# Routing by expert choice: a threshold search on two engines instead of one

## The chip, the cores and the metric

The kernel runs on one core of a Trainium2 chip. Its engines are TensorE (PE in the profile: matmuls, with PEld for weight loads), VectorE (DVE), ScalarE (ACT), GpSimd (POOL) and SyncE (SP, which issues DMAs). They run their own instruction streams and meet at semaphores. The metric is the device time of one execution in microseconds, the median of some runs.

## The reference

The program is one transformer layer on 4096 tokens of 256 features: linear attention with random features, a feed-forward block, and a mixture of 8 experts. The part that matters here is how the experts choose their tokens. `x` has 8 x 512 tokens:

```
scores = softmax(xf @ gate_w.T, axis=-1)        # 4096 tokens x 8 experts
vals, idx = top_k(scores.T, k)                  # k = 4096 / 8 = 512 tokens for each expert
y = xf[idx]                                     # gathered rows, normalised
h = gelu(y @ fc1[e].T + b1[e]);  out = (h @ fc2[e].T + b2[e]) * vals
xf = xf.at[idx].add(out)                        # scattered back
x = x + layernorm(xf)
```

So for each expert the 512 largest of 4096 scores are wanted, exactly, and ties at the threshold go to the first tokens.

## The kernel before, in words

Everything is one launch, written by hand with one instruction stream for each engine and named semaphores between them. First come eight batches of 512 tokens through attention, feed-forward and gate, as a software pipeline of three stages; `batches` writes batches 0 to 2 and the tail as straight-line code and the middle ones as a hardware loop. Then comes the selection, then `experts`: expert 0, a loop over the middle ones, and the last two. At the end the sum is normalised and written.

The selection works like this. The gate's scores lie in `sc`; TensorE turns them (L1353) into PSUM tile `pA[0]`, so that each of the 128 partitions holds 256 scores: 16 partitions for each of the 8 experts. VectorE copies them to `S` (L1098), which lies in the free buffer `kp`, and makes a bfloat16 copy of their upper halves, `S_hi` (L1101). A score is positive, so its f32 bits as an integer are in the same order as the score. The search settles three bits of the threshold in each of ten rounds. In a round

- VectorE counts, for each of 7 candidates, how many scores of the partition are at least the candidate (L1108, a compare with an accumulator, so each is followed by a read of the accumulator); the first four rounds use `S_hi`, the other six `S`;
- TensorE sums the counts over the 16 partitions of an expert with the 0/1 matrix `blockones` (L1627) into `pA[1]`;
- VectorE compares the sums with 512 (L1115), scales the number of candidates that passed by the step (L1117), and makes the next 7 candidates (L1118), the threshold so far (L1119) and the next step (L1120). `Steps.link` puts a wait behind an instruction, so the next one starts only when it is done; `Steps.put` doesn't.

On VectorE the rounds are two hardware loops with two rounds in a body, on TensorE one loop. Behind the search VectorE counts once more, above the cut and equal to it (L1131, L1132), and turns the counts into places, one-hot matrices and at last row numbers `idx` (to L1176). GpSimd then gathers the rows of expert 0 (L799), and only then can expert 0 start: TensorE turns the rows (L1353), ScalarE applies the layer norm's scale and shift (L616, Identity), and the first hidden products follow (L1382), with Gelu on ScalarE (L630).

What sets the order of the work around the search: SyncE issues the weights of expert 0 (`kp<-fc1T`, `w<-fc2T`, 1 MB each) as soon as the last batch's buffers are free, and the following experts' weights behind `idx_ready`. GpSimd wrote the selection's constants once, in front of the batches (`selection_constants`, from L673). ScalarE has nothing to do between the last batch and L616.

Of the kernel before, what the change touches and what calls it, by code (L numbers as in the profile page):

```python
# [6 lines left out]
ALU = mybir.AluOpType  # L7
# [10 lines left out]
P = 128  # L18
# [11 lines left out]
EPS_K = 1e-4  # L30
N_CONST = 14
N_WFF = 13
N_SEL = 13
LN_EPS = 1e-5
LNS = 5
NORM = DH ** -0.25
# [5 lines left out]
ROW = D + E  # L42
GT = KEEP // P

ROUNDS, CANDS = 10, 7
HI_ROUNDS = 4
SA, SB = 32, 16
SR = P // SA
LQ = 4
# [48 lines left out]
def build(nc, video, WqT, bq, WkT, bk, WvT, bv, WoT, bo, projT, W1T, b1, W2T, b2, g2, be2, g3, be3,  # L98
          gateT, ln_w, ln_b, fc1T, b1s, fc2T, b2s, out, stop=None):
    with ExitStack() as ctx:  # L100
# [10 lines left out]
        def features_of(t):  # L111
# [83 lines left out]

        kp_f, qe_f, qp_f = (a[:].rearrange("p a b -> p (a b)") for a in (kp, qe, qp))
        S, gt, eq, gin, ein, place = (kp_f[:, k * SEGW:(k + 1) * SEGW] for k in range(6))
        flags = qe_f[:, 8 * SEGW:(8 + CANDS) * SEGW].rearrange("p (k j) -> p k j", k=CANDS)

        flags_hi, S_hi = (qe_f[:, k * SEGW:(k + w) * SEGW].bitcast(BF16) for k, w in ((8, CANDS // 2 + 1), (15, 1)))  # L200
        flags_hi, S_hi = flags_hi[:, 0:CANDS * SEGW].rearrange("p (k j) -> p k j", k=CANDS), S_hi[:, 0:SEGW]
        dig_a, dig_b = (kp_f[:, 7 * SEGW:8 * SEGW].bitcast(F16)[:, k * SEGW:(k + 1) * SEGW].rearrange("p (e c s) -> p e c s", c=C, e=E)
                        for k in range(2))
        placei, digi_a, digi_b = (qe_f[:, k * SEGW:(k + 1) * SEGW].bitcast(I32).rearrange("p (c e s) -> p c e s", c=C, e=E)
                                  for k in (8, 9, 10))
        thr = sb("thr", [P, 1], U32)
        step = sb("step", [P, CANDS], U32)
        nstep = sb("nstep", [P, CANDS], U32)
        base = sb("base", [P, CANDS], U32)
        cand = sb("cand", [P, CANDS], U32)  # L210
        cnt = sb("cnt", [P, CANDS])
        passed = sb("passed", [P, CANDS])
        npass = sb("npass", [P, 1])
        up = sb("up", [P, 1], U32)
        ones_row = sb("ones_row", [P, SEGW])
        blockones = sb("blockones", [P, P])
        blockbelow = sb("blockbelow", [P, P])
# [94 lines left out]
        x1_out, xf_out, y_out, sc_out = sem("x1_out"), sem("xf_out"), sem("y_out"), sem("sc_out")  # L312
        dve_n, dve_a, dve_f, dve_u = sem("dve_n"), sem("dve_a"), sem("dve_f"), sem("dve_u")
        sel_const, sel_step, s_turned, s_ready = sem("sel_const"), sem("sel_step"), sem("s_turned"), sem("s_ready")
        cnt_ready, tot_ready, dve_s, dve_r = sem("cnt_ready"), sem("tot_ready"), sem("dve_s"), sem("dve_r")
        pair_ready, off_ready, place_ready, place_turned = sem("pair_ready"), sem("off_ready"), sem("place_ready"), sem("place_turned")
        oneb_ready, onea_ready, onehot_ready, ids_ready, rbd_ready, spread_ready, idx_ready = (
            sem("oneb_ready"), sem("onea_ready"), sem("onehot_ready"), sem("ids_ready"), sem("rbd_ready"), sem("spread_ready"), sem("idx_ready"))
# [10 lines left out]
            sem("olv_ready"), sem("olp_ready"))  # L329

        STEPS_N, STEPS_A, STEPS_F, STEPS_U = 1, 7, 1, 7
        SEL_STEPS = 7

        vid_d = video.rearrange("(b t p) d -> b p t d", t=TT, p=P)
        x1_t = x1_d.rearrange("(b t p) d -> b p t d", t=TT, p=P)
# [125 lines left out]
        def _(act):  # L461
# [188 lines left out]
        def _(pool):  # L650
# [21 lines left out]
            def selection_constants():  # L672
                nc.gpsimd.memset(ones_row[:], 1.0).then_inc(sel_const, 1)  # L673
                nc.gpsimd.memset(zero4[:], 0.0).then_inc(sel_const, 1)

                for k in range(CANDS):
                    nc.gpsimd.memset(step[:, k:k + 1], (k + 1) << 27).then_inc(sel_const, 1)
                nc.gpsimd.memset(thr[:], 0).then_inc(sel_const, 1)

                for m in (blockones, blockbelow, spread, rmask):  # L680
                    nc.gpsimd.memset(m[:], 1.0).then_inc(sel_step, 1)
                nc.gpsimd.iota(iota_row[:], [[1, SA]], base=0, channel_multiplier=0).then_inc(sel_step, 1)
                pool.wait_ge(sel_step, 5)
# [165 lines left out]
        def _(dve):  # L849
# [244 lines left out]
            done.link(nc.vector.tensor_scalar(pmod[:], pint[:], SR - 1, None, ALU.bitwise_and))  # L1094
            done.link(nc.vector.tensor_copy(pmodf[:], pmod[:]))
            done.link(nc.vector.tensor_scalar(rmask[:], iotaf[:, 0:SR], pmodf[:, 0:1], None, ALU.is_equal))
            dve.wait_ge(s_turned, 1)
            nc.vector.tensor_copy(S, pA[0][:, 0:SEGW]).then_inc(s_ready, 1)  # L1098
            dve.wait_ge(s_ready, 1)

            done.link(nc.vector.tensor_copy(S_hi, S.bitcast(BF16).rearrange("p (j h) -> p j h", h=2)[:, :, 1]))  # L1101

            def search(rd, s, fl):


                ss = Steps(dve, dve_r, SEL_STEPS, rd)
                for k in range(CANDS):
                    nc.vector.tensor_scalar(fl[:, k], s, cand[:, k:k + 1].bitcast(F32), None, ALU.is_ge, ALU.add,  # L1108
                                            accum_out=cnt[:, k:k + 1]).then_inc(cnt_ready, 1)

                ss.link(nc.vector.tensor_scalar(nstep[:], step[:], 3, None, ALU.logical_shift_right))
                ss.put(nc.vector.tensor_tensor(base[:], nstep[:], thr[:].to_broadcast([P, CANDS]), ALU.bitwise_or))
                dve.wait_ge(tot_ready, rd + 1)

                ss.link(nc.vector.tensor_scalar(passed[:], pA[1][:, 0:CANDS], KEEP - 0.5, None, ALU.is_ge, ALU.add,  # L1115
                                                accum_out=npass[:]))
                ss.link(nc.vector.tensor_scalar(up[:], step[:, 0:1], npass[:, 0:1], None, ALU.mult))  # L1117
                ss.put(nc.vector.tensor_tensor(cand[:], base[:], up[:].to_broadcast([P, CANDS]), ALU.bitwise_or))  # L1118
                ss.put(nc.vector.tensor_tensor(thr[:], thr[:], up[:], ALU.bitwise_or))  # L1119
                ss.link(nc.vector.tensor_copy(step[:], nstep[:]))  # L1120
                ss.end()

            done.link(nc.vector.tensor_copy(cand[:], step[:]))
            with dve.Fori(0, HI_ROUNDS // 2) as r2:
                search(r2 * 2, S_hi, flags_hi)
                search(r2 * 2 + 1, S_hi, flags_hi)
            with dve.Fori(HI_ROUNDS // 2, ROUNDS // 2) as r2:
                search(r2 * 2, S, flags)
                search(r2 * 2 + 1, S, flags)
            cut = thr[:, 0:1].bitcast(F32)  # L1130
            nc.vector.tensor_scalar(gt, S, cut, None, ALU.is_gt, ALU.add, accum_out=pair_cnt[:, 0:1])  # L1131
            nc.vector.tensor_scalar(eq, S, cut, None, ALU.is_equal, ALU.add, accum_out=pair_cnt[:, 1:2]).then_inc(pair_ready, 1)  # L1132
            dve.wait_ge(pair_ready, 1)
            nc.vector.tensor_tensor_scan(gin, ones_row[:], gt, 0.0, ALU.mult, ALU.add)
            nc.vector.tensor_tensor_scan(ein, ones_row[:], eq, 0.0, ALU.mult, ALU.add)
# [157 lines left out]
        def _(pe):  # L1293
# [436 lines left out]
```

## Time and profile before

| | us |
|---|---|
| median of 3 runs | 970.05 (969.35 to 970.36) |
| the profiled execution, its own time | 970.41 |
| its span, first to last instruction | 968.6 |
| busy: PE 762.2, DVE 595.6, ACT 410.6, POOL 352.9 | |
| mean granted TensorE clock | 0.900 of full speed |

The stages follow each other: batches to about 630, the search to 677, placing to 698, gather and the turning of the first rows to 715, experts to about 929, the last normalisation to the end. The page cuts the span into 40 slices of 24.2 us; a digit is the busy share of an engine in a slice, in tenths. The busy share of an engine over the whole span says little about a single stage; the rows below are read by stage.

### The profile page before, as it was taken

How to read it: one execution, taken by the hardware profiler on the slowest of the kernel's cores; microseconds unless marked ns; L12 is line 12 of the kernel's file. 1: busy time of each engine (PE TensorE's matmuls, PEld its weight loads, DVE VectorE, ACT ScalarE, POOL GpSimd, SP SyncE). 2: the span in 40 equal slices, each digit the busy share in tenths (PEclk: the TensorE clock that was granted, in tenths of full speed). 3: DMA queues.
4: the chain of work that ended last, by engine and by line, in shares of the span. 5: the costliest groups of instructions: out<-in, count | busy, mean ns of one | idle time of the engine just before them, and what ended most of it. 6: DMA issues, size and time to landing. Idle time of an engine off the chain costs nothing.

```text
span 968.6 us, 15201 instructions
## 1 busy us (share of the span) xinstructions
PE 762.2 (79%) x5561; PEld 581.5 (60%) x5561; DVE 595.6 (61%) x1426; ACT 410.6 (42%) x594; POOL 352.9 (36%) x299
## 2 busy tenths in 40 slices
PE   5578999999999999999999967211459989999900
PEld 2345856767767758668577656211348888888800
DVE  2722735857857957848758562588836656666445
ACT  2632634735636536637447321100045434455324
POOL 3136333514416405425335151100134444544346
PEclk9798999999999999999999979555569999999955
DMA  7000010011011020110100102220053555555274
GB/s 208 1 23 1 1 45 1 2 66 46 23 44 44 22 84 3 48 61 0 65 23 1 66 23 83 71 94 0 7 169 92 153 132 170 138 132 135 31 213 150
DMA packets 61530, 64.63 MB, mean 67 GB/s; under 512 B 9264, under 2 KB 58160, under 8 KB 61488
## 3 DMA queue, kind: packets, MB, share of 16 engines
q1 hardware_dynamic: 54384, 55.37, 17.4%
q0 software_dynamic: 6144, 8.52, 5.0%
q8 instruction: 27, 0.44, 0.2%
q10 hardware_dynamic: 960, 0.17, 0.1%
q14 instruction: 15, 0.12, 0.0%
HBM read 42.95 MB, written 21.10 MB: 66 GB/s over the span
## 4 chain that ended last, share of the span: by engine, by line
PE 62%; DVE 13%; DMA 6%; ACT 6%; POOL 6%; issue 5%; POOLq 0%; DVEq 0%; SPq 0%; ACTq 0%
PE pF L1382 10%; PE pX L1660 10%; PE pF L1424 9%; PE pA L1368 6%; PE pA L1375 5%; PE pX L1464 5%; DMA xg<-row_scratch,idx_g 4%; PE pX L1393 4%; PE pA L1353 3%; DVE qe L1108 3%; PE pX L1382 3%; POOL xg L799 2%; PE pA L1434 2%; PE pF L1477 2%; PE pF L1353 2%
## 5 line engine op out<-in xcount | busy, mean ns | idle before, releaser
L1424 PE MATMUL pF<-w,h 128*128 128x256 f32 x512 | 116.0, 380 | 0.0
L1424 PEld LDWEIGHTS pF<-w,h 128*128 128x128 f32 x512 | 95.6, 190 | 13.8 <-issue 1.4
L719 POOL TENSOR_SCALAR ve<-mv 128x4 f32<-128x4 f32 x40 | 9.1, 228 | 247.0 <-DVE mv L861 246.4
L807 POOL DMA_INDIRECT acc_scratch<-at,idx_s x32 | 51.6, 1613 | 107.3 <-DVE at L1216 100.6
L799 POOL DMA_INDIRECT xg<-row_scratch,idx_g x32 | 47.3, 1478 | 99.0 <-issue 86.0
L630 ACT ACTIVATE h<-pX,b1cur 128x512 f32<-128x512 f32 x64 | 44.1, 690 | 88.9 <-DVE b1cur L1227 75.4
L1660 PE MATMUL pX<-w_lo,h_hi 128*128 128x256 f32 x256 | 73.7, 288 | 0.8 <-issue 0.8
L1660 PE MATMUL pX<-w_hi,h_lo 128*128 128x256 f32 x256 | 73.0, 285 | 0.0
L1660 PE MATMUL pX<-w_hi,h_hi 128*128 128x256 f32 x256 | 72.9, 285 | 0.0
L867 DVE TENSOR_SCALAR z<-z,mv,rstd 128x256 f32<-128x256 f32 x64 | 62.3, 1034 | 7.0 <-POOL rstd L721 7.0
L479 ACT ACTIVATE h<-pF,b1c 128x512 f32<-128x512 f32 x64 | 44.2, 691 | 48.4 <-PE pF L1382 48.4
L1199 DVE TENSOR_TENSOR h_lo<-h,h_hi 128x512 fp32r<-128x512 f32 x64 | 42.9, 690 | 30.5 <-ACT h_hi L622 30.5
L1382 PE MATMUL pF<-x2T_hi,w_lo 128*128 128x512 f32 x128 | 55.1, 430 | 1.4 <-DVE x2T_lo L957 1.4
L1382 PE MATMUL pX<-x2T_hi,w_lo 128*128 128x512 f32 x128 | 51.8, 405 | 2.8 <-DVE x2T_lo L1248 2.8
L1382 PE MATMUL pX<-x2T_lo,w_hi 128*128 128x512 f32 x128 | 51.6, 403 | 0.0
L1382 PE MATMUL pF<-x2T_hi,w_hi 128*128 128x512 f32 x128 | 51.5, 403 | 0.0
L1382 PE MATMUL pX<-x2T_hi,w_hi 128*128 128x512 f32 x128 | 51.4, 401 | 0.0
L1382 PE MATMUL pF<-x2T_lo,w_hi 128*128 128x512 f32 x128 | 51.2, 400 | 0.0
L1660 PEld LDWEIGHTS pX<-w_lo,h_hi 128*128 128x128 f32 x256 | 49.7, 194 | 1.4 <-issue 1.4
L888 DVE TENSOR_REDUCE mxk<-kp 128x16 f32<-128x1024 f32 x32 | 37.3, 1209 | 21.4 <-ACT kp L489 21.4
L1660 PEld LDWEIGHTS pX<-w_hi,h_lo 128*128 128x128 f32 x256 | 49.7, 194 | 0.0
L1660 PEld LDWEIGHTS pX<-w_hi,h_hi 128*128 128x128 f32 x256 | 49.6, 194 | 0.0
(260 smaller groups left out, 1860.0 us busy)
## 6 DMA issues: line engine op xcount, KB each, us to landing
kp<-fc1T SPq DMA_DIRECT2D x8, 1024.0 KB, 7.9
w<-fc2T SPq DMA_DIRECT2D x8, 1024.0 KB, 8.0
xin<-video SPq DMA_DIRECT2D x8, 512.0 KB, 3.9
x<-video SPq DMA_DIRECT2D x8, 512.0 KB, 4.5
x_scratch<-x SPq DMA_DIRECT2D x8, 512.0 KB, 2.9
acc_scratch<-xf SPq DMA_DIRECT2D x8, 512.0 KB, 3.0
row_scratch<-y SPq DMA_DIRECT2D x8, 512.0 KB, 3.0
qp<-x_scratch SPq DMA_DIRECT2D x2, 1024.0 KB, 10.5
```

The source lines that it names most:

```text
L479: nc.scalar.activation(dst, pF[n % 2][:], func, **kw).then_inc(done, 1)
L630: nc.scalar.activation(h[:, n, :], pM[n % M_SLOTS], ACT.Gelu_apprx_tanh, bias=b1cur[:, n:n + 1]).then_inc(he_ready, 1)
L799: pool.indirect_dma_start(xg[:, g, :], None, row_d, bass.IndirectOffsetOnAxis(ap=idx_g[:, g:g + 1], axis=0)).then_inc(gathered, 16)
L807: pool.indirect_dma_start(acc_d, bass.IndirectOffsetOnAxis(ap=idx_s[:, g:g + 1], axis=0), og[:, g, :], None, compute_op=ALU.add).then_inc( ...
L867: ins = nc.vector.tensor_scalar(dst[:, t, :], src[:, t, :], mv[k][:, t, 0:1], rstd[k][:, t:t + 1], ALU.subtract, ALU.mult)
L1353: return nc.tensor.transpose(dst, src, ident[:])
L1368: ins = nc.tensor.matmul(dst[:, t2 * D:(t2 + 1) * D], xt[:, k, tok(2 * m + t2)], w[:, k, :], start=(k == 0), stop=(k == ks - 1))
L1375: ins = nc.tensor.matmul(dst[:], w[:, k, tok(n)], xt[:, k, :], start=(k == 0), stop=(k == ks - 1))
L1382: ins = nc.tensor.matmul(dst[:], w_[:, k, tok(n)], x_[:, k, :], start=(m == 0), stop=(m == len(parts) - 1))
L1424: ins = nc.tensor.matmul(slots[m][:, half * D:(half + 1) * D], h[:, k, tok(2 * m + half)], w2[:, k, :], start=(k == 0), stop=(k == FC - 1))
L1464: ins = nc.tensor.matmul(pXall[:, a, :], w_[rows], x_[rows], start=(n == 0), stop=(n == 2), tile_position=(32 * a, 0))
L1660: ins = nc.tensor.matmul(pM[2 + m][:, t2 * D:(t2 + 1) * D], h_[:, k, tok(2 * m + t2)], w_[:, k, :], start=(k == 0 and j == 0), stop=(k == ...
```

## The change

The search still settles three bits in each of ten rounds, with 7 candidates. What differs:

- The scores become numbers. The upper bits of the score (shifted right by 15) are cast to f32 as `S_top` and searched in rounds 0 to 4; then the low 15 bits, scaled by 2^-15, are joined to what is left of `S_top` above the threshold found, and this `S` is searched in rounds 5 to 9. Candidates lie half a step between the values, so none is ever equal to a score.
- VectorE counts 4 candidates (scores below the candidate), ScalarE 3, as the sum of Sign(candidate - score) over the row, with an accumulator. For a sum of signs the limit differs; the limits stand in `limit`.
- The decision is a compare with `limit`, a reduce, one instruction for the next candidates (which ScalarE awaits, `cand_ready`), and one for the threshold `below`. The first candidates of each half are made before the search.
- TensorE waits for both engines' counts (`cnt_ready`, `sgn_ready`).
- The rounds are straight-line code on VectorE, ScalarE and TensorE.
- ScalarE runs one small Sign before the search and one small Gelu behind it, into `spare`.
- GpSimd sets four small constants where it set eight.

```diff
-ROUNDS, CANDS = 10, 7
-HI_ROUNDS = 4
+ROUNDS, CANDS, CANDS_V = 10, 7, 4
+HI_ROUNDS = ROUNDS // 2
+LOW_BITS = 15
+STEP = [float(1 << 3 * (HI_ROUNDS - 1 - r)) for r in range(HI_ROUNDS)] + [2.0 ** (-3 * (r + 1)) for r in range(HI_ROUNDS)]
+BELOW = (-0.5, -0.5 * STEP[ROUNDS - 1])
...
+            act.wait_ge(sel_const, N_SEL)
+            nc.scalar.activation(spare[:], zero4[:, 0:1], ACT.Sign)
+            for rd in range(ROUNDS):
+                act.wait_ge(s_ready, 1 if rd < HI_ROUNDS else 3)
+                act.wait_ge(cand_ready, rd + 1 if rd < HI_ROUNDS else rd)
+                now = cand_low if rd == HI_ROUNDS else cand
+                for j in range(CANDS - CANDS_V):
+                    k = CANDS_V + j
+                    nc.scalar.activation(signs[:, j], S_top if rd < HI_ROUNDS else S, ACT.Sign, bias=now[:, k:k + 1], scale=-1.0,
+                                         accum_out=cnt[:, k:k + 1]).then_inc(sgn_ready, 1)
+            nc.scalar.activation(spare[:], zero4[:, 0:1], ACT.Gelu_apprx_tanh)
...
-                for k in range(CANDS):
-                    nc.gpsimd.memset(step[:, k:k + 1], (k + 1) << 27).then_inc(sel_const, 1)
-                nc.gpsimd.memset(thr[:], 0).then_inc(sel_const, 1)
+                for k in range(2):
+                    nc.gpsimd.memset(thr[:, k:k + 1], BELOW[k]).then_inc(sel_const, 1)
+
+                nc.gpsimd.memset(limit[:, 0:CANDS_V], SEG * SEGW - KEEP + 0.5).then_inc(sel_const, 1)
+                nc.gpsimd.memset(limit[:, CANDS_V:CANDS], SEG * SEGW - 2 * KEEP + 0.5).then_inc(sel_const, 1)
...
+            nc.vector.tensor_scalar(cand[:], iotaf[:, 1:CANDS + 1], STEP[0], BELOW[0], ALU.mult, ALU.add).then_inc(cand_ready, 1)
+            done.link(nc.vector.tensor_scalar(cand_low[:], iotaf[:, 1:CANDS + 1], STEP[HI_ROUNDS], BELOW[1], ALU.mult, ALU.add))
             dve.wait_ge(s_turned, 1)
-            nc.vector.tensor_copy(S, pA[0][:, 0:SEGW]).then_inc(s_ready, 1)
+            done.link(nc.vector.tensor_scalar(bits_top, pA[0][:, 0:SEGW].bitcast(I32), LOW_BITS, None, ALU.arith_shift_right))
+            nc.vector.tensor_copy(S_top, bits_top).then_inc(s_ready, 1)
             dve.wait_ge(s_ready, 1)
...
+            ss = Steps(dve, dve_r, 0, 0)
+            for rd in range(ROUNDS):
+                half = rd // HI_ROUNDS
+                last_of_half = rd % HI_ROUNDS == HI_ROUNDS - 1
+                scores, now = S if half else S_top, cand_low if rd == HI_ROUNDS else cand
+                below = thr[:, half:half + 1]
+                for k in range(CANDS_V):
+                    nc.vector.tensor_scalar(flags[:, k], scores, now[:, k:k + 1], None, ALU.is_lt, ALU.add,
+                                            accum_out=cnt[:, k:k + 1]).then_inc(cnt_ready, 1)
+                if rd == 0:
+                    done.link(nc.vector.tensor_scalar(bits_low, pA[0][:, 0:SEGW].bitcast(I32), (1 << LOW_BITS) - 1, None, ALU.bitwise_and))
+                    nc.vector.tensor_scalar(S_low, bits_low, 2.0 ** -LOW_BITS, BELOW[0], ALU.mult, ALU.add).then_inc(s_ready, 1)
+                if not last_of_half:
+                    ss.link(nc.vector.tensor_scalar(kstep[:], iotaf[:, 1:CANDS + 1], STEP[rd + 1], below, ALU.mult, ALU.add))
                 dve.wait_ge(tot_ready, rd + 1)
+                ss.link(nc.vector.tensor_tensor(passed[:], pA[1][:, 0:CANDS], limit[:], ALU.is_le))
+                ss.link(nc.vector.tensor_reduce(npass[:], passed[:], AX_X, ALU.add))
+                if not last_of_half:
+                    nc.vector.scalar_tensor_tensor(out=cand[:], in0=npass[:].to_broadcast([P, CANDS]), scalar=STEP[rd], in1=kstep[:],
+                                                   op0=ALU.mult, op1=ALU.add).then_inc(cand_ready, 1)
+                ss.link(nc.vector.tensor_scalar(below, npass[:], STEP[rd], below, ALU.mult, ALU.add))
+                if rd == HI_ROUNDS - 1:
+                    dve.wait_ge(s_ready, 2)
+                    nc.vector.scalar_tensor_tensor(out=S, in0=S_top, scalar=below, in1=S_low, op0=ALU.subtract, op1=ALU.add).then_inc(s_ready, 1)
+                    dve.wait_ge(s_ready, 3)
+                elif not last_of_half:
+                    dve.wait_ge(cand_ready, rd + 2 if rd < HI_ROUNDS else rd + 1)
+            done.link(nc.vector.tensor_scalar(cut[:], thr[:, 1:2], BELOW[1], None, ALU.subtract))
...
-            with pe.Fori(0, ROUNDS) as rd:
-                pe.wait_ge(cnt_ready, (rd + 1) * CANDS)
+            for rd in range(ROUNDS):
+                pe.wait_ge(cnt_ready, (rd + 1) * CANDS_V)
+                pe.wait_ge(sgn_ready, (rd + 1) * (CANDS - CANDS_V))
                 nc.tensor.matmul(pA[1][:, 0:CANDS], blockones[:], cnt[:], start=True, stop=True).then_inc(tot_ready, 1)
```

## Rows read from the trace of the kernel before

**Rows 1.** The page, the span in 40 slices of 24.2 us.
```profile
DVE  2722735857857957848758562588836656666445
ACT  2632634735636536637447321100045434455324
PEclk9798999999999999999999979555569999999955
```

**Rows 2.** Busy us (instructions): PE, PEld, DVE, ACT, POOL; then clock, DMA share, GB/s.
```profile
631.00:677.00 46.00, 5.95 (x20) 5.01 (x20) 38.51 (x221) 0.00 (x0) 0.00 (x0) 0.50 0.14 49
```

**Rows 3.** Timeline of VectorE in rounds 5 to 7: start, duration, line; and the search's end.
```profile
649.95 0.48 DVE L1108 TENSOR_SCALAR_CACHE_REDUCE qe<-kp,cand 128x256 f32<-128x256 f32 x1 [0.38 <-DVE step L1120]
650.35 0.08 DVE L1108 DVE_READ_ACCUMULATOR qe<-kp,cand 128x1 f32 x1
...
652.75 0.09 DVE L1108 DVE_READ_ACCUMULATOR qe<-kp,cand 128x1 f32 x1
...
653.52 0.17 DVE L1115 TENSOR_SCALAR_CACHE_REDUCE passed<-pA 128x7 f32<-128x7 f32 x1 [0.40 <-PE pA L1627]
...
653.73 0.22 DVE L1117 TENSOR_SCALAR up<-step,npass 128x1 uint32<-128x1 uint32 x1
653.98 0.17 DVE L1118 TENSOR_TENSOR cand<-base,up 128x7 uint32<-128x7 uint32 x1
654.06 0.15 DVE L1119 TENSOR_TENSOR thr<-thr,up 128x1 uint32<-128x1 uint32 x1
...
654.33 0.48 DVE L1108 TENSOR_SCALAR_CACHE_REDUCE qe<-kp,cand 128x256 f32<-128x256 f32 x1
...
659.12 0.48 DVE L1108 TENSOR_SCALAR_CACHE_REDUCE qe<-kp,cand 128x256 f32<-128x256 f32 x1 [0.44 <-DVE step L1120]
...
677.23 0.48 DVE L1131 TENSOR_SCALAR_CACHE_REDUCE kp<-kp,thr 128x256 f32<-128x256 f32 x1 [0.23 <-DVE step L1120]
```

**Rows 4.** Timeline of VectorE at the start of the search.
```profile
630.14 0.42 DVE L1098 COPY kp<-pA 128x256 f32<-128x256 f32 x1
630.60 0.29 DVE L1101 COPY qe<-kp 128x256 bf16<-128x256 bf16 x1
...
631.35 0.48 DVE L1108 TENSOR_SCALAR_CACHE_REDUCE qe<-qe,cand 128x256 bf16<-128x256 bf16 x1 [0.25 <-DVE cand L1123]
```

**Rows 5.** VectorE's groups by form: count, busy us, mean ns of one, idle before.
```profile
L1117 DVE TENSOR_SCALAR up<-step,npass 128x1 uint32<-128x1 uint32 x10 | 2.1, 215 | 0.4
...
L1144 DVE SCALAR_TENSOR_TENSOR kp<-kp,offs 128x256 f32<-128x256 f32 x1 | 0.5, 485 | 0.0
...
L1043 DVE TENSOR_REDUCE lmx<-lg 128x4 f32<-128x32 f32 x2 | 0.4, 186 | 0.1
```

**Rows 6.** ScalarE's groups by form over the span, same columns.
```profile
L538 ACT ACTIVATE y<-x,ny,ry 128x256 f32<-128x256 f32 x32 | 16.6, 588 | 61.3 <-DVE ny L1003 55.8 <-issue 5.5
...
L474 ACT ACTIVATE kT<-pA,bqk 128x512 f32<-128x512 f32 x16 | 11.0, 687 | 52.0 <-PE pA L1375 52.0
...
L474 ACT ACTIVATE v<-pA 128x512 f32<-128x512 f32 x16 | 9.6, 597 | 17.3 <-PE pA L1368 17.3
...
L603 ACT ACTIVATE lg<-lg 128x32 f32<-128x32 f32 x8 | 1.8, 231 | 7.3 <-DVE lg L1044 7.3
```

**Rows 7.** Timeline of ScalarE behind the search.
```profile
711.71 0.78 ACT L616 ACTIVATE aT<-pX,lnb_c,lnw_c 128x512 f32<-128x512 f32 x1 [83.02 <-PE pX L1353]
...
718.33 1.28 ACT L630 ACT_TABLE_LOAD   x1 [3.85 <-PE pX L1382]
719.63 0.69 ACT L630 ACTIVATE h<-pX,b1cur 128x512 f32<-128x512 f32 x1
```

**Rows 8.** DMAs from 625 to 700: issues, KB each, us to landing.
```profile
w<-fc2T SPq DMA_DIRECT2D x1, 1024.0 KB, 7.9
```

**Rows 9.** The chain of waits from 610 to 740: start, duration.
```profile
715.35 13.61 PE pX L1382 x48
```

**Rows 10.** Who waited for whom: us in total, times, the longest.
```profile
DVE st L857 <- issue: 0.9, 3, 0.3
```

More of the change, by code:

```diff
@@ L32 @@
 N_WFF = 13
-N_SEL = 13
+N_SEL = 9
 LN_EPS = 1e-5
@@ L197, in build @@
         S, gt, eq, gin, ein, place = (kp_f[:, k * SEGW:(k + 1) * SEGW] for k in range(6))
-        flags = qe_f[:, 8 * SEGW:(8 + CANDS) * SEGW].rearrange("p (k j) -> p k j", k=CANDS)
-        flags_hi, S_hi = (qe_f[:, k * SEGW:(k + w) * SEGW].bitcast(BF16) for k, w in ((8, CANDS // 2 + 1), (15, 1)))
-        flags_hi, S_hi = flags_hi[:, 0:CANDS * SEGW].rearrange("p (k j) -> p k j", k=CANDS), S_hi[:, 0:SEGW]
+        S_top, S_low = (kp_f[:, k * SEGW:(k + 1) * SEGW] for k in (6, 4))
+        flags = qe_f[:, 8 * SEGW:(8 + CANDS_V) * SEGW].rearrange("p (k j) -> p k j", k=CANDS_V)
+        signs = qe_f[:, (8 + CANDS_V) * SEGW:15 * SEGW].rearrange("p (k j) -> p k j", k=CANDS - CANDS_V)
+        bits_top, bits_low = (kp_f[:, k * SEGW:(k + 1) * SEGW].bitcast(I32) for k in (1, 2))
         dig_a, dig_b = (kp_f[:, 7 * SEGW:8 * SEGW].bitcast(F16)[:, k * SEGW:(k + 1) * SEGW].rearrange("p (e c s) -> p e c s", c=C, e=E)
@@ L205, in build @@
                                   for k in (8, 9, 10))
[L206 to L210, printed above, removed]
+        thr = sb("thr", [P, 2])
+        kstep = sb("kstep", [P, CANDS])
+        cand = sb("cand", [P, CANDS])
+        cand_low = sb("cand_low", [P, CANDS])
+        limit = sb("limit", [P, CANDS])
+        cut = sb("cut", [P, 1])
+        spare = sb("spare", [P, 1])
         cnt = sb("cnt", [P, CANDS])
@@ L213, in build @@
         npass = sb("npass", [P, 1])
-        up = sb("up", [P, 1], U32)
         ones_row = sb("ones_row", [P, SEGW])
@@ L314, in build @@
         sel_const, sel_step, s_turned, s_ready = sem("sel_const"), sem("sel_step"), sem("s_turned"), sem("s_ready")
-        cnt_ready, tot_ready, dve_s, dve_r = sem("cnt_ready"), sem("tot_ready"), sem("dve_s"), sem("dve_r")
+        cnt_ready, sgn_ready, tot_ready, dve_s, dve_r, cand_ready = (
+            sem("cnt_ready"), sem("sgn_ready"), sem("tot_ready"), sem("dve_s"), sem("dve_r"), sem("cand_ready"))
         pair_ready, off_ready, place_ready, place_turned = sem("pair_ready"), sem("off_ready"), sem("place_ready"), sem("place_turned")
@@ L331, in build @@
         STEPS_N, STEPS_A, STEPS_F, STEPS_U = 1, 7, 1, 7
-        SEL_STEPS = 7
         vid_d = video.rearrange("(b t p) d -> b p t d", t=TT, p=P)
@@ L1099, in _ @@
+            nc.vector.tensor_copy(S_top, bits_top).then_inc(s_ready, 1)
             dve.wait_ge(s_ready, 1)
[L1101 to L1108, printed above, removed]
-                                            accum_out=cnt[:, k:k + 1]).then_inc(cnt_ready, 1)
-                ss.link(nc.vector.tensor_scalar(nstep[:], step[:], 3, None, ALU.logical_shift_right))
-                ss.put(nc.vector.tensor_tensor(base[:], nstep[:], thr[:].to_broadcast([P, CANDS]), ALU.bitwise_or))
-                dve.wait_ge(tot_ready, rd + 1)
[L1115 to L1131, printed above, removed]
@@ L1132, in _ @@
-            nc.vector.tensor_scalar(eq, S, cut, None, ALU.is_equal, ALU.add, accum_out=pair_cnt[:, 1:2]).then_inc(pair_ready, 1)
+            ss = Steps(dve, dve_r, 0, 0)
[6 more added lines that the diff above has]
+                    nc.vector.tensor_scalar(flags[:, k], scores, now[:, k:k + 1], None, ALU.is_lt, ALU.add,
+                                            accum_out=cnt[:, k:k + 1]).then_inc(cnt_ready, 1)
+                if rd == 0:
[3 more added lines that the diff above has]
+                    ss.link(nc.vector.tensor_scalar(kstep[:], iotaf[:, 1:CANDS + 1], STEP[rd + 1], below, ALU.mult, ALU.add))
+                dve.wait_ge(tot_ready, rd + 1)
+                ss.link(nc.vector.tensor_tensor(passed[:], pA[1][:, 0:CANDS], limit[:], ALU.is_le))
[10 more added lines that the diff above has]
+                    dve.wait_ge(cand_ready, rd + 2 if rd < HI_ROUNDS else rd + 1)
@@ L1133, in _ @@
+            done.link(nc.vector.tensor_scalar(cut[:], thr[:, 1:2], BELOW[1], None, ALU.subtract))
+            nc.vector.tensor_scalar(gt, S, cut[:, 0:1], None, ALU.is_gt, ALU.add, accum_out=pair_cnt[:, 0:1])
+            nc.vector.tensor_scalar(eq, S, cut[:, 0:1], None, ALU.is_equal, ALU.add, accum_out=pair_cnt[:, 1:2]).then_inc(pair_ready, 1)
             dve.wait_ge(pair_ready, 1)
@@ L1622, in _ @@
             ins.then_inc(s_turned, 1)
-            with pe.Fori(0, ROUNDS) as rd:
-                pe.wait_ge(cnt_ready, (rd + 1) * CANDS)
+            for rd in range(ROUNDS):
+                pe.wait_ge(cnt_ready, (rd + 1) * CANDS_V)
+                pe.wait_ge(sgn_ready, (rd + 1) * (CANDS - CANDS_V))
                 nc.tensor.matmul(pA[1][:, 0:CANDS], blockones[:], cnt[:], start=True, stop=True).then_inc(tot_ready, 1)
             pe.wait_ge(pair_ready, 1)
-            pe.wait_ge(s_ready, 1)
+            pe.wait_ge(s_ready, 2)
             nc.tensor.matmul(pA[0][:, 0:2], blockbelow[:], pair_cnt[:], start=True, stop=True)
```

## The prediction

> **What bounds the kernel now.** I read the page's slices first, then the busy times by stage, then the timeline of the search, then the rows of the engine that is to take work over. The slices show, near two thirds of the span, VectorE at 8 and ScalarE at 0 with TensorE's granted clock at 5 [rows 1]. The stage gives its size [rows 2]: in the 46 us from 631 to 677 VectorE is busy 38.5 us, TensorE 6, ScalarE and GpSimd nothing. That is the threshold search: one dependent chain through VectorE and TensorE, so every microsecond of it is a microsecond of the span, and all later work (placing, gather, experts) starts from its result.
>
> One round [rows 3]: the first count starts at 649.95; the reads of the first and the seventh accumulator stand at 650.35 and 652.75, six spacings, so counts follow each other by 0.40, and the last is read at 652.84: 2.89 = 6 x 0.40 + 0.49. TensorE's block sum and its way back take 0.68, to L1115 at 653.52. The decision (L1115, L1117 to L1120) takes 0.81, to the next count at 654.33: 4.38 us in all. Every second round also turns the loop: 659.12 lies 4.79 behind 654.33, with 0.44 idle in front of it. Ten rounds go from 631.35 [rows 4] to the count for the cut at 677.23 [rows 3].
>
> **The change, part by part.** All of it is counted on this chain.
>
> (a) Three of seven counts leave VectorE. Four take 3 x 0.40 + 0.49 = 1.69, 1.20 less per round. The bfloat16 copy of the scores goes too; it bought nothing: a count of it lasts 0.48 [rows 4], one of f32 0.48 [rows 3].
>
> (b) The decision. L1115's replacement is a compare of 7 columns without an accumulator, as short as L1118 (0.17 [rows 3]), and then a reduce; the nearest reduce is 186 ns for 32 columns [rows 5]. A dependent instruction starts some 0.04 behind its predecessor (L1118 behind L1117 [rows 3]), so each takes 0.21. The next candidates are one instruction, 0.17. Behind them the new base, one column with a pointer scalar like L1117 (215 ns [rows 5]), may start 0.08 after the candidates, as L1119 does behind L1118 [rows 3], and is awaited. So the counts start 0.42 + 0.08 + 0.22 + 0.04 = 0.76 behind the compare, where it is 0.81 now. kstep stands before the wait for TensorE and fits beside its 0.68.
>
> (c) No loop turn: the pause of about 0.4 in every second round goes.
>
> A round of VectorE is then 0.76 + 1.69 + 0.68 = 3.13 us.
>
> (d) ScalarE's three signs. It has candidates 0.42 + 0.17 + 0.03 = 0.62 behind the compare. No row has a Sign with an accumulator. The nearest is the 128x256 activation with two pointer operands: 588 ns, 16.6 us for 32 busy, so 0.52 each where they overlap [rows 6]. One pointer less saves 687 - 597 = 90 ns [rows 6]. So a Sign lasts 0.50 and follows by 0.43 at most, and I take 0.42. Lower bound of the three: 2 x 0.42 + 0.50 = 1.34, the accumulator free. Upper bound: each also pays a separate read as dear as the shortest activation, 231 ns [rows 6], and nothing overlaps: 3 x (0.50 + 0.23) = 2.19. The nearest row in kind is VectorE's read of an accumulator, 0.08 [rows 3]; it gives 1.34 + 3 x 0.08 = 1.58, and that I take. ScalarE is then ready 0.62 + 1.58 = 2.20 behind the compare and VectorE 0.76 + 1.69 = 2.45: ScalarE is hidden by 0.25. It comes last only if the three take more than 1.83.
>
> (e) Start. Two tables of candidates stand in front of the wait for the turned scores: up to 0.08 + 0.17 + 0.04 = 0.29, and I hide nothing of it. The shift starts at 630.43 instead of 630.14 [rows 4]; from PSUM it costs L1098's 0.42 + 0.04, the cast L1101's 0.29 + 0.05. First count: 631.23, against 631.35 now.
>
> (f) First round: between counts and decision stand the low 15 bits (0.46, from PSUM), their scaling (0.27) and kstep (0.27): 1.00 where 0.68 would do, so +0.32. Middle: behind the fifth decision the scores are put together once, with a pointer scalar (485 ns at L1144 [rows 5]): 0.21 + 0.21 + 0.26 + 0.53 = 1.21 instead of 0.76, so +0.45. End: 0.21 + 0.21 + 0.26 + 0.19 = 0.87 to the count for the cut.
>
> Sum: first compare at 631.23 + 1.69 + 0.68 + 0.32 = 633.92; nine rounds more, 9 x 3.13 + 0.45 = 28.62, to 662.54; + 0.87 gives 663.41. Now it is 677.23, so 13.8 us go.
>
> (g) Side work at nothing. TensorE runs the same ten sums, with a second wait in front of each; what is queued behind each is only the next sum. GpSimd sets constants once, ahead of the batches, four small ones fewer; its next work there waits for other engines, so I take 0. ScalarE was idle for 83.02 us before its first instruction behind the search, at 711.71 [rows 7]; 30 signs and two small activations in about 34 us fit there, and only that instruction is queued behind them. Expert 0's weights (1 MB in 7.9 us [rows 8]) are issued at the start of the search and needed behind it: some 20 us of cover stay even if they wait for each other.
>
> (h) The Gelu table. Now its load of 1.28 us stands before the first hidden activation, at 718.33 [rows 7]; the spare Gelu moves it behind the search. I count no gain: TensorE's 48 matmuls of that stretch stand in the chain of waits as one piece of 13.61 us from 715.35 on, without a wait for ScalarE [rows 9]. Between -1.3 and 0, I take 0. Whether Sign is in the table now loaded (it serves Copy, Relu, Square and Exp) no row shows; if not, the spare Sign costs from 0 to 1.3 once, less what lies between ScalarE's last exponential and the first candidate; I take 0.
> The Trainium skill, "ScalarE: Activation LUTs", section "What ACT_TABLE_LOAD costs", puts a drain of some 1.38 us on top of the 1.28. Here the next activation starts at 719.63, 0.02 behind the load [rows 7]: measurement and page differ. By the page each warm-up would end 1.4 later; the Gelu's would still lie inside the idle 83 us and the sum would stay, while a Sign in a table of its own would cost up to 2.7 once.
>
> The profiled execution took 970.41 (span 968.6), the median run 970.05. From the profiled one the sum is 956.6, from the median 956.2. Every term is at its row's shortest spacing, so I predict 956.6.
>
> **Rivals.**
> 1. ScalarE comes last. For it: the accumulator's price is unseen, and the margin is 0.25 in 3.1. Against: only a read dearer than about 0.16 decides it. At the upper bound a round is 0.62 + 2.19 + 0.68 = 3.49, so 8 x 0.36 + 0.5 in the middle + 0.2 in the first = 3.6 us of the gain go: 960.2.
> 2. An exposed instruction fetch. The search was a loop on VectorE and TensorE and becomes straight-line code on three engines, while 2 MB of weights are in flight. For it: a transfer among those weights takes 7.9 us to land [rows 8]. Against: the longest idle time of VectorE put down to issue is 0.3 us in the whole span [rows 10], though four of eight batches run as straight-line code. One exposed fetch costs up to 7.9: up to 964.5.
> 3. Slower than before: two such fetches, both within the transfer of the weights and both on the chain, on engines that wait for each other. The price is 2 x 7.9 = 15.8 against 13.8 gained: 972.4. It decides from 6.9 us per fetch; nothing in the trace comes near it.
> 4. The search shortens, but the gain is given back by what follows: the gather, or TensorE's clock. Against: the gather needs only rows that were written before the search, and the granted clock is 5 from the search through the gather either way [rows 1]. The time would be 970.
>
> **How the numbers follow.** Forecast 0.58; rival 1 in some measure 0.28; rival 2 0.09; rival 3 0.03; rival 4 0.02. The range is 955.0 to 961.5: below, the load of 1.3 counted as no gain, and 0.3 for the start; above, ScalarE's upper bound and a small stall. A measurement tells 0.2% (1.9 us) from no change; forecast and rivals 1 and 2 are faster, and of rival 2 a hundredth is worse: 0.94; no change 0.02; slower 0.04.
>
> **What would show it.** In the changed profile: first counts of two rounds 3.13 apart (3.5 by rival 1); TensorE's idle time before the sums put down to VectorE's count, not to ScalarE's sign; Sign rows near 0.50, the last one ended before VectorE's fourth count; the count for the cut 13.8 earlier; no row of the experts changed; the table load near 663. I am wrong if TensorE waits for ScalarE, if the rounds have idle time put down to issue, or if a load appears between signs.

## The result, and the profile after

The changed kernel takes 956.77 us (median of 4 runs, 953.76 to 959.91); the kernel before took 970.2 beside it (4 runs). The ratio is 0.9862, 95% interval 0.9829 to 0.9895. Predicted were 956.6 and a range of 955.0 to 961.5. The profiled execution took 959.91, its span is 957.8.

The same slices as in [rows 1], now 23.9 us each. ScalarE has two 4s where it had 0s behind the batches, and the row of TensorE's clock has one 5 fewer there:

```profile
DVE  2631634875866857857957754657636656566445
ACT  1542553744745635635546513044045434455424
PEclk9789899999999999999999989655569999999955
```

The stage of the search, with the columns of [rows 2]. It is 33 us long where it was 46; TensorE has the same 20 passes in it, ScalarE 62 instructions where it had none:

```profile
633.00:666.00 33.00, 5.95 (x20) 5.01 (x20) 26.04 (x133) 17.32 (x62) 0.00 (x0) 0.52 0.21 70
```

One round, as [rows 3] showed one: start and duration, all engines, from one compare to the next. VectorE and ScalarE read the same scores at the same time, and neither is slower for it: a count lasts 0.48 as in [rows 3], and a Sign lasts 0.49, as the fourth Sign of split_3_4 does with no count beside it:

```profile
639.55 0.17 DVE L1141 TENSOR_TENSOR passed<-pA,limit 128x7 f32<-128x7 f32 x1 [0.62 <-PE pA L1651]
639.75 0.16 DVE L1142 TENSOR_REDUCE npass<-passed 128x1 f32<-128x7 f32 x1
639.94 0.17 DVE L1144 SCALAR_TENSOR_TENSOR cand<-npass,kstep 128x7 f32<-128x7 f32 x1
640.03 0.21 DVE L1146 TENSOR_SCALAR thr<-npass,thr 128x1 f32<-128x1 f32 x1
640.20 0.51 ACT L625 ACTIVATE qe<-kp,cand 128x256 f32<-128x256 f32 x1 [1.58 <-DVE cand L1144]
640.27 0.48 DVE L1132 TENSOR_SCALAR_CACHE_REDUCE qe<-kp,cand 128x256 f32<-128x256 f32 x1
640.62 0.19 ACT L625 ACTIVATION_READ_ACCUMULATOR qe<-kp,cand 128x1 f32 x1
...
640.71 0.49 ACT L625 ACTIVATE qe<-kp,cand 128x256 f32<-128x256 f32 x1
...
641.20 0.49 ACT L625 ACTIVATE qe<-kp,cand 128x256 f32<-128x256 f32 x1
...
641.60 0.19 ACT L625 ACTIVATION_READ_ACCUMULATOR qe<-kp,cand 128x1 f32 x1
641.87 0.08 DVE L1132 DVE_READ_ACCUMULATOR qe<-kp,cand 128x1 f32 x1
641.87 0.23 DVE L1139 TENSOR_SCALAR kstep<-iotaf,thr 128x7 f32<-128x7 f32 x1
642.01 0.59 PE L1651 MATMUL pA<-cnt,blockones 128*128 128x7 f32 x2 [2.57 <-DVE qe L1132]
642.71 0.17 DVE L1141 TENSOR_TENSOR passed<-pA,limit 128x7 f32<-128x7 f32 x1 [0.61 <-PE pA L1651]
```

ScalarE's last read ends at 641.79, VectorE's at 641.95, and TensorE starts at 642.01. The waits say the same: before all ten sums TensorE waited for VectorE, never for ScalarE (us in total, times, the longest).

```profile
PE pA L1651 <- DVE qe L1132: 26.4, 10, 2.9
```

The start of the selection, the start of the search and its end, which answer to [rows 4] and the last row of [rows 3], and the table load behind it:

```profile
632.15 0.15 DVE L1113 TENSOR_SCALAR pmod<-pint 128x1 int32<-128x1 int32 x1
...
633.07 0.42 DVE L1120 TENSOR_SCALAR kp<-pA 128x256 int32<-128x256 int32 x1
633.53 0.29 DVE L1121 CAST kp<-kp 128x256 f32<-128x256 int32 x1
633.86 0.48 DVE L1132 TENSOR_SCALAR_CACHE_REDUCE qe<-kp,cand 128x256 f32<-128x256 f32 x1
...
664.35 1.28 ACT L627 ACT_TABLE_LOAD   x1
665.64 0.20 ACT L627 ACTIVATE spare<-zero 128x1 f32<-128x1 f32 x1
666.02 0.48 DVE L1155 TENSOR_SCALAR_CACHE_REDUCE kp<-kp,cut 128x256 f32<-128x256 f32 x1
```

For all kernels I take the search as the time from the first instruction of the selection (pmod, a fixed point in every version) to the count for the cut. Here it is 666.02 - 632.15 = 33.87 us. In the kernel before the same instruction stood at 629.44:

```profile
629.44 0.15 DVE L1094 TENSOR_SCALAR pmod<-pint 128x1 int32<-128x1 int32 x1
```

so the search took 677.23 - 629.44 = 47.79, and 13.92 us of it are gone. But this execution reached the selection 2.71 us later than that one, 0.4 us are lost behind the search, and 0.3 lie outside the span. So only 10.5 us lie between the two profiled executions; between the medians it is 13.4. The experiments show what those 2.71 us are.

### The profile page after: what moved, and what is told of

Its sections match the earlier page's. It is cut to its first block, busy times and chain, and to the rows that moved or that the text cites. A ratio compares the mean times of both kernels' runs of the same rounds, so it can differ in the third digit from the quotient of the medians.

```text
span 957.8 us, 15109 instructions
## 1 busy us (share of the span) xinstructions
PE 766.5 (80%) x5561; PEld 584.4 (61%) x5561; DVE 582.5 (61%) x1337; ACT 426.5 (45%) x656; POOL 353.2 (37%) x295
## 4 chain that ended last, share of the span: by engine, by line
PE 64%; DVE 13%; ACT 6%; POOL 6%; DMA 5%; issue 4%; POOLq 0%; DVEq 0%; ACTq 0%; SPq 0%
PE pF L1406 10%; PE pX L1684 10%; PE pF L1448 9%; PE pA L1392 6%; PE pA L1399 5%; PE pX L1488 5%; DMA xg<-row_scratch,idx_g 4%; PE pX L1406 4%; PE pX L1417 4%; PE pA L1377 3%; POOL xg L818 2%; PE pA L1458 2%; ACT qp L534 2%; DVE qe L1132 2%; PE pF L1501 2%
## 5 line engine op out<-in xcount | busy, mean ns | idle before, releaser
L1448 PEld LDWEIGHTS pF<-w,h 128*128 128x128 f32 x512 | 95.6, 190 | 13.8 <-issue 1.4
## 6 DMA issues: line engine op xcount, KB each, us to landing
qp<-x_scratch SPq DMA_DIRECT2D x2, 1024.0 KB, 10.5
```

The costliest lines, as they stand in the source:

```text
L1448: ins = nc.tensor.matmul(slots[m][:, half * D:(half + 1) * D], h[:, k, tok(2 * m + half)], w2[:, k, :], start=(k == 0), stop=(k == FC - 1))
```

## The experiments

Each ratio is against the kernel before, timed beside the run: its median was 970.2 for the changed kernel, 970.15 for the runs from changed_again to unroll_only, 970.97 for those from no_gelu_preload to f16_and_base and 969.61 for the last two. "Search" is the stretch just defined; "selection starts" is its first instruction in the profiled execution.

| kernel | median us | ratio, 95% interval | search | selection starts |
|---|---|---|---|---|
| before | 970.15 | | 47.79 | 629.44 |
| changed | 956.77 | 0.9862 (0.9829 to 0.9895) | 33.87 | 632.15 |
| changed_again | 956.69 | 0.9855 (0.9838 to 0.9873) | 33.80 | 631.86 |
| split_7_0 | 968.19 | 0.9981 (0.9967 to 0.9994) | 45.86 | 629.26 |
| split_3_4 | 960.45 | 0.9891 (0.9873 to 0.9908) | 37.91 | 632.34 |
| unroll_only | 967.03 | 0.9974 (0.9955 to 0.9992) | 45.53 | 633.52 |
| no_gelu_preload | 955.76 | 0.9853 (0.9831 to 0.9876) | 33.84 | 631.13 |
| base_not_awaited | 955.88 | 0.9847 (0.9830 to 0.9863) | 32.95 | 630.90 |
| sum_in_f16 | 952.45 | 0.9820 (0.9798 to 0.9842) | 30.21 | 628.63 |
| f16_and_base | 952.43 | 0.9813 (0.9799 to 0.9826) | 29.38 | 631.01 |
| kstep_not_awaited | 957.57 | 0.9870 (0.9850 to 0.9891) | 33.21 | 631.72 |
| all_three | 951.58 | 0.9819 (0.9806 to 0.9833) | 28.77 | 630.77 |

The searches lie 19 us apart. The median less the search is 921.5 to 924.4 in all twelve rows, and 921.5 to 923.1 without kstep_not_awaited: the search accounts for the differences of the medians to that measure.

**changed_again** has no edit.

> The changed kernel once more, for its own spread and for a second trace. Theory A (the whole change of time is the search; the two profiled executions differ by 2.7 us before it because TensorE's clock rose later in the first batch, by chance): the stretch from the shift of the scores to the count for the cut is again 32.95 us, while the time of single executions scatters over some us; median near 956.3. Rival (the change itself delays the batches): the batches end near 631 again and not near 628.5 as in the kernel before.

The search is 33.80, and the median agrees with the first measurement. The selection starts at 631.86, which by itself would speak for the rival; unroll_only decides that below.

**split_7_0**: all seven counts on VectorE. ScalarE's Signs, their limit and TensorE's wait for them are taken out too.

```diff
-ROUNDS, CANDS, CANDS_V = 10, 7, 4
+ROUNDS, CANDS, CANDS_V = 10, 7, 7
...
```

> The changed kernel with all seven counts on VectorE and no Sign on ScalarE. Theory A (what the engines share is what pays): three counts more per round, 3 x 0.40 = 1.20, so 12.0 us more, near 968.5, a round of 4.37. Rival (the shorter decision and the missing loop turns pay, the sharing little): under 962.

```profile
629.26 0.15 DVE L1101 TENSOR_SCALAR pmod<-pint 128x1 int32<-128x1 int32 x1
...
675.12 0.48 DVE L1143 TENSOR_SCALAR_CACHE_REDUCE kp<-kp,cut 128x256 f32<-128x256 f32 x1
```

The search is 45.86, so 11.99 us longer than 33.87, and the time is 968.19. The sharing is worth 12.0 us, as three counts of 0.40 in ten rounds are; the rival falls.

**split_3_4**: three counts on VectorE, four Signs on ScalarE.

```diff
-ROUNDS, CANDS, CANDS_V = 10, 7, 4
+ROUNDS, CANDS, CANDS_V = 10, 7, 3
```

> The changed kernel with three counts on VectorE and four signs on ScalarE. Theory A (ScalarE sits just below the point where it decides): four signs end 0.65 + 3 x 0.495 + 0.39 + 0.19 = 2.72 behind the compare, so TensorE waits for ScalarE and a round is 2.72 + 0.69 = 3.41 instead of 3.17: some 2.4 us slower than the changed kernel, near 959. Rival (ScalarE has room, VectorE decides): 0.40 less per round, some 4 us faster, near 952.5.

The sign of the expectation was right and its size too small: 3.8 us slower than the changed kernel, not 2.4; a round is 3.55, not 3.41. The timeline of a round, from its reduce on:

```profile
640.88 0.16 DVE L1142 TENSOR_REDUCE npass<-passed 128x1 f32<-128x7 f32 x1 [0.23 <-DVE passed L1141]
...
642.60 0.09 DVE L1132 DVE_READ_ACCUMULATOR qe<-kp,cand 128x1 f32 x1
...
643.22 0.19 ACT L625 ACTIVATION_READ_ACCUMULATOR qe<-kp,cand 128x1 f32 x1
643.52 0.50 PEld L1651 LDWEIGHTS pA<-cnt,blockones 128*128 128x128 f32 x2 [3.24 <-DVE qe L1132]
643.55 0.56 PE L1651 MATMUL pA<-cnt,blockones 128*128 128x7 f32 x2 [3.18 <-ACT qe L625]
644.22 0.17 DVE L1141 TENSOR_TENSOR passed<-pA,limit 128x7 f32<-128x7 f32 x1 [1.39 <-PE pA L1651]
```

VectorE is done at 642.69 and ScalarE at 643.41. The weight load starts 0.11 behind ScalarE's read, where it started 0.05 to 0.06 behind VectorE's in the changed kernel, and the compare 0.81 behind the read. The four Signs took what I expected; the 0.69 that I put behind them should have been 0.81. In this one round the reduce also starts 0.20 late (0.23 behind the compare, elsewhere 0.03), which makes the round 3.74 and is 0.2 of the 4.04 that the search grew by; what held it up is open. One Sign more, and ScalarE decides: the split of 4 and 3 is the best of those tried.

**unroll_only**: the kernel before, with its ten rounds written out.

```diff
-            with dve.Fori(0, HI_ROUNDS // 2) as r2:
-                search(r2 * 2, S_hi, flags_hi)
-                search(r2 * 2 + 1, S_hi, flags_hi)
...
+            for rd in range(ROUNDS):
+                search(rd, *((S_hi, flags_hi) if rd < HI_ROUNDS else (S, flags)))
...
-            with pe.Fori(0, ROUNDS) as rd:
+            for rd in range(ROUNDS):
```

> The kernel before with its ten rounds written out on VectorE and TensorE, nothing else. Theory A (a loop turn costs 0.4 on VectorE in every second round and nothing replaces it): four turns, 1.7 us less in the search, 968.4. Rival (straight-line code has fetches that are exposed): as before or slower, 970 to 978, with idle time put down to issue in the rounds.

```profile
639.60 0.48 DVE L1108 TENSOR_SCALAR_CACHE_REDUCE qe<-qe,cand 128x256 bf16<-128x256 bf16 x1
...
643.99 0.48 DVE L1108 TENSOR_SCALAR_CACHE_REDUCE qe<-qe,cand 128x256 bf16<-128x256 bf16 x1
```

Every round is now 4.38 or 4.39 long. The search is 2.26 us shorter, where 1.7 were expected: four turns of some 0.4, and 0.2 each at the first count, in the first decision and at the count for the cut (the 0.23 idle in the last line of [rows 3]). No idle time stands in its rounds that the loop version lacked. It also answers the question of changed_again. Its batches are the code of the kernel before, yet its selection starts at 633.52, the latest of all, while split_7_0 and sum_in_f16, which have the new selection, start it at 629.26 and 628.63. The granted clock in the first batches goes with it. From 20 to 150 us it is 0.91 in the three executions that start the selection before 630 (before, split_7_0, sum_in_f16), 0.89 in the eight that start it between 630.77 and 632.34, and 0.88 in unroll_only at 633.52. Most of unroll_only's loss stands in the first 40 us of that stretch (columns of [rows 2]; first the kernel before, then unroll_only):

```profile
20.00:60.00 40.00, 26.63 (x305) 16.50 (x307) 19.09 (x30) 21.76 (x24) 10.64 (x6) 0.83 0.00 1
```

```profile
20.00:60.00 40.00, 27.47 (x301) 17.41 (x300) 17.85 (x27) 21.76 (x24) 10.65 (x6) 0.77 0.02 6
```

So the start of the selection scatters over 5 us between executions, and the change isn't needed for it. What makes the clock rise earlier or later in an execution stays open, and so does why the kernel before scattered less (16 runs within 2.9 us) than unroll_only (10 runs within 8.7).

**no_gelu_preload**: the changed kernel without the spare Gelu.

```diff
-            nc.scalar.activation(spare[:], zero4[:, 0:1], ACT.Gelu_apprx_tanh)
```

> The changed kernel without the spare Gelu behind the search. Theory A (the table load was hidden beside TensorE's 48 matmuls anyway): the load of 1.28 stands again before the first Gelu of expert 0, which starts 1.2 later, and the time is that of the changed kernel, 956.7, within its spread. Rival (the load was on the path): 1.2 slower, 958.

The load is back before the first Gelu, with 3.85 idle in front as in [rows 7], and the time is not longer than the changed kernel's (955.76). Here are the first two Gelus without the preload, then with it:

```profile
706.19 1.28 ACT L646 ACT_TABLE_LOAD   x1 [3.85 <-PE pX L1405]
707.49 0.69 ACT L646 ACTIVATE h<-pX,b1cur 128x512 f32<-128x512 f32 x1
708.55 0.69 ACT L646 ACTIVATE h<-pX,b1cur 128x512 f32<-128x512 f32 x1 [0.38 <-PE pX L1405]
```

```profile
707.27 0.69 ACT L647 ACTIVATE h<-pX,b1cur 128x512 f32<-128x512 f32 x1 [3.87 <-PE pX L1406]
709.61 0.69 ACT L647 ACTIVATE h<-pX,b1cur 128x512 f32<-128x512 f32 x1 [1.65 <-PE pX L1406]
```

Counted from the count for the cut (664.97 and 666.02), the first Gelu comes at 42.52 and at 41.25, but the second at 43.58 and 43.59: it waits for TensorE either way. TensorE's 48 matmuls of that stretch take 13.73 us in the chain of waits of both. No gain came from the preload, and the load cost nothing on the path.

**base_not_awaited**: VectorE's counts no longer wait for the new base.

```diff
+                    ss.sync()
                     ss.link(nc.vector.tensor_scalar(kstep[:], iotaf[:, 1:CANDS + 1], STEP[rd + 1], below, ALU.mult, ALU.add))
...
-                ss.link(nc.vector.tensor_scalar(below, npass[:], STEP[rd], below, ALU.mult, ALU.add))
+                (ss.link if last_of_half else ss.put)(nc.vector.tensor_scalar(below, npass[:], STEP[rd], below, ALU.mult, ALU.add))
```

> The changed kernel, but VectorE's counts no longer wait for the new base; only the next step does, behind the counts. Theory A (VectorE comes last by about 0.1): the counts start 0.21 instead of 0.32 behind the candidates, VectorE's last read is then 0.21 + 1.69 = 1.90 behind them and ScalarE's 0.26 + 1.58 = 1.84, so both meet and a round is 3.06: 0.9 us less, 955.8. Rival (ScalarE's signal reaches TensorE later than VectorE's and decides at once): less than 0.4 us less.

A round is 3.05 or 3.06, the search 32.95: 0.92 less, and the median 0.8 less, within the scatter. It was the search that told the theories apart. The two engines meet, as expected: in the round whose weight load starts at 643.58, VectorE's last read ends at 643.51, 0.07 before it, and ScalarE's at 643.46, some 0.11 before it, which is what split_3_4 showed where ScalarE decided.

**sum_in_f16**: the counts and the 0/1 matrices in float16.

```diff
-        cnt = sb("cnt", [P, CANDS])
+        cnt = sb("cnt", [P, CANDS], F16)
...
-        blockones = sb("blockones", [P, P])
-        blockbelow = sb("blockbelow", [P, P])
-        pair_cnt = sb("pair_cnt", [P, 2])
+        blockones = sb("blockones", [P, P], F16)
+        blockbelow = sb("blockbelow", [P, P], F16)
+        pair_cnt = sb("pair_cnt", [P, 2], F16)
```

> The changed kernel with the counts, the pair counts and the two 0/1 matrices in float16 (all counts are whole numbers up to 256), so that the block sum is one pass of TensorE at half clock instead of two. Theory A (the sum is on the path of every round): the 0.59 of the two f32 passes becomes about 0.29, as the f16 product behind the placing took; 0.3 less in each of ten rounds and 0.6 less behind the search, 953.2. Rival (the way from TensorE to VectorE is mostly fixed): 1 us or less, 955.7 or more.

It gave more than expected in the rounds: 0.40 each, 2.76 or 2.77 instead of 3.17, because the product takes 0.19 and not the 0.29 that I had from a wider one.

```profile
638.37 0.17 DVE L1142 TENSOR_TENSOR passed<-pA,limit 128x7 f32<-128x7 f32 x1 [0.21 <-PE pA L1652]
...
640.84 0.19 PE L1652 MATMUL pA<-cnt,blockones 128*128 128x7 f16 x1 [2.58 <-DVE qe L1133]
641.14 0.17 DVE L1142 TENSOR_TENSOR passed<-pA,limit 128x7 f32<-128x7 f32 x1 [0.21 <-PE pA L1652]
```

The 0.6 behind the search did not come: from the cut to the row numbers it is 20.6 us as before, since the sums there run beside VectorE's scans (in the changed kernel the first of them starts at 666.96, the scan at 666.94). The search is 30.21, 3.66 less; the median is 4.2 less than the changed kernel's 956.69, and by the ratios it is 3.4.

**f16_and_base**: both edits.

> Both edits together, the float16 sums and the counts that do not wait for the base. Theory A: they touch different parts of the round and add up, 3.5 + 0.9 less, near 952.3, faster than the kernel before and the changed one. Rival (ScalarE decides once VectorE starts earlier): the sum of float16 alone.

The search is 29.38: 3.66 and 0.92 would be 4.58, measured are 4.49. The median, 952.43, does not separate it from sum_in_f16.

**kstep_not_awaited**: in the changed kernel the compare came 0.11 behind the end of TensorE's sum (642.60 to 642.71 above), in [rows 3] 0.04 (the sum ended at 653.48). This edit takes the wait behind kstep away; the wait behind the compare covers both.

```diff
-                    ss.link(nc.vector.tensor_scalar(kstep[:], iotaf[:, 1:CANDS + 1], STEP[rd + 1], below, ALU.mult, ALU.add))
+                    ss.put(nc.vector.tensor_scalar(kstep[:], iotaf[:, 1:CANDS + 1], STEP[rd + 1], below, ALU.mult, ALU.add))
```

> The changed kernel, but VectorE does not wait for kstep in front of its wait for TensorE; the wait behind the compare covers both. In the changed kernel the compare starts 0.11 behind the end of the sum in the eight rounds with kstep and 0.04 in the two without. Theory A (the sequencer handles the two waits one after the other, and the first one is what makes the second late): 0.07 less in eight rounds, a round of 3.10, the search from 33.87 to 33.3; the total within its spread. Rival (the compare is late for another reason, such as its second operand): 3.17 as before.

```profile
641.37 0.59 PE L1651 MATMUL pA<-cnt,blockones 128*128 128x7 f32 x2 [2.50 <-DVE qe L1132]
642.00 0.17 DVE L1141 TENSOR_TENSOR passed<-pA,limit 128x7 f32<-128x7 f32 x1 [0.54 <-PE pA L1651]
```

The compare now stands 0.04 behind the sum, a round is 3.09 or 3.10, the search 33.21. The median is 957.57, a little above the changed kernel's: two thirds of a microsecond are not to be seen in it.

**all_three**: the edits of sum_in_f16, base_not_awaited and kstep_not_awaited together.

> Float16 sums, counts that do not wait for the base, and kstep not awaited. In the float16 kernels the time from VectorE's last read to the compare is near 0.37, within which a kstep of 0.23 and its wait just fit. Theory A: 0.07 less in eight rounds, 2.59 a round, the search from 29.38 to 28.8, total near 951.9. Rival (nothing is left there, ScalarE's signal decides): 2.66 as in the kernel with two edits.

A round is 2.59 and the search 28.77, both as expected. At 951.58 it has the lowest median here, but the kernel before was also faster beside it (969.61 against 970.97): the ratio of 0.9819 does not separate it from f16_and_base (0.9813) or sum_in_f16 (0.9820). All_three and f16_and_base are faster than the changed kernel beyond the interval of changed_again (0.9833 and 0.9826 at the upper ends, against 0.9838 at its lower end); against the first measurement of the changed kernel, whose interval starts at 0.9829, only f16_and_base is.

## Why the prediction was right

**The bound.** The search was one chain, and what left it left the span. The 13.9 us went through to the end; nothing behind the search gave any back that other executions don't give back too. From the count for the cut to the end of the span it is 291.4 us before and 291.8 in the changed kernel, and 287.7 to 291.8 in the other ten.

**(a) Three counts per round, 1.20.** In the profile four counts take 1.68 (640.27 to 641.95) against 1.69 predicted, and split_7_0 measured the sharing at 11.99 us.

**(b) The decision.** 0.72 from the compare to the counts (639.55 to 640.27), predicted 0.76. Against that, the way from VectorE's last read to the compare is 0.76, predicted 0.68 from the kernel before. I said that kstep fits beside it; it does, but the wait behind kstep, which I left out of the sum, makes the next one late by 0.07, as kstep_not_awaited shows. The two errors leave a round at 3.17 instead of 3.13.

**(c) The loop turns.** In unroll_only the search is 2.26 us shorter. So the 13.92 are 2.26 from the loops, 11.99 from the sharing, and -0.33 from everything else: the search on numbers with its two joints costs a little more than the one on bits (45.86 in split_7_0 against 45.53 in unroll_only). Some 0.6 of the 2.26 are the three pauses of 0.2 that the prediction did not name; they lay in the measured stretch that it started from.

**(d) The three Signs.** Taken at 1.58, measured 1.59 (640.20 to 641.79), but partly by luck. The price of the read, 0.08, was VectorE's; ScalarE's lasts 0.19. It fits only because the next Sign starts 0.09 into the read, so that Signs follow each other by 0.49 to 0.51, where 0.42 and the read had made 0.50, and because the last read begins 0.40 behind the start of its Sign and not 0.50. By the prediction's own words a read dearer than 0.16 would have let ScalarE decide; that held only for reads that overlap nothing. The groups by form:

```profile
L625 ACT ACTIVATE qe<-kp,cand 128x256 f32<-128x256 f32 x27 | 13.4, 497 | 15.0 <-DVE cand L1144 12.6 <-DVE kp L1121 2.4
L625 ACT ACTIVATION_READ_ACCUMULATOR qe<-kp,cand 128x1 f32 x27 | 5.0, 186 | 0.0
```

ScalarE's first Sign starts 0.65 behind the compare (0.62 predicted), and ScalarE ends 0.16 before VectorE, predicted 0.25. Rival 1 was therefore near: split_3_4 shows it at work.

**(e), (f) Start, joints and end.** The two tables of candidates cost 0.22 (predicted up to 0.29): the shift stands 0.92 behind the first instruction of the selection, the copy of the kernel before 0.70. From the shift to the first count 0.79 (predicted 0.80). The first compare stands 0.84 behind the last read (1.00), the joint costs 0.44 more than a normal round (3.61 against 3.17; predicted 0.45), the end takes 0.84 (0.87). From the shift to the count for the cut it is 32.95 in all; the sum of the prediction gives 32.98.

**(g), (h) Side work.** TensorE's sums wait for VectorE alone; no load stands before or between the Signs, so Sign is in the table in use, and only the Gelu's load remains, at 664.35. It starts 0.02 behind the last Sign's read. There the next activation starts at 665.64, 0.01 behind the load: again no trace of the drain that the Trainium skill, "ScalarE: Activation LUTs", section "What ACT_TABLE_LOAD costs", names. The preload changed nothing but the first Gelu, as no_gelu_preload shows.

**Rivals 2 and 3** (exposed fetches): the rounds of the changed kernel are all 3.16 or 3.17 apart outside the joints (3.09 or 3.10 into the two decisions that have no kstep), and those of unroll_only 4.38 or 4.39, so none holds a stall. The one pause of 0.2 in split_3_4 is the only one seen in straight-line rounds here, far below the 7.9 that the rival was priced at. **Rival 4**: from the row numbers to ScalarE's first instruction of expert 0 it is 13.9 us before (697.85 to 711.71) and 14.0 after (686.64 to 700.64), and the 48 matmuls take 13.61 and 13.73.

What the prediction did not have is the scatter. It assumed that a measurement tells 0.2% (1.9 us) from no change; single executions of the changed kernel lie 6 us apart. The agreement of the total to 0.2 us is therefore chance. That of the search (13.92 against 13.8) is not, though it is closer than its parts: the nine rounds took 28.80 against 28.62, and the first compare came 2.52 behind the first count against 2.69, which nearly cancel.

## What to carry to other kernels

This chain of small dependent rounds could be priced from the profile to some 1%, with no part off by more than 0.2 us: take spacings, not durations, and count the waits in front of a wait. When an idle engine can take over part of such a round, split the work so that the engine with the dearer handoff ends a little earlier. Then look at what is left between the engines: here the way the sums were stored (two passes in f32, one in float16) was worth 3.7 us, more than the other two edits behind the change (0.9 and 0.7).

Where executions scatter by more than the effect, measure the stretch in the trace from a fixed instruction to another; edits of 0.6 to 0.9 us were plain there and invisible in the medians.

## What the runs showed of the hardware that was not expected

- A Sign with an accumulator on ScalarE is two instructions, 497 and 186 ns for 128x256, and the next one starts 0.09 into the read, so they follow each other by 0.49.
- Where VectorE waited for its own kstep and directly behind it for TensorE, the compare came 0.11 behind the sum; with the first wait gone, 0.04 (kstep_not_awaited). The first wait cost 0.07, though it had been met long before the sum ended.
- TensorE's weight load started 0.11 behind ScalarE's last read when ScalarE came last (split_3_4) and 0.05 to 0.06 behind VectorE's when VectorE did. The two waits stand one behind the other on TensorE, ScalarE's second; whether the order or the engine makes the difference was not tried. The second wait costs nothing when it is met first: in split_7_0, which has only the one for VectorE, the load starts 0.06 behind the read too (642.67 to 642.73).
- At the granted clock of 0.50 a float16 product of 7 columns took 0.19 (sum_in_f16), where f32 takes two passes and 0.59.
